# A cross-attention, state-space and feed-forward kernel: the loads for the first two tiles of the modulation stage leave a wait for TensorE's count of turned tiles

## What is computed

```
xt = ln(x)
scores = (xt Wq)(ctx Wk)^T / sqrt(32)        # 4 heads, top 32 of 3202 kept, softmax over these
c_t    = (mean over heads of attn) (ctx Wv)  # context of each token
h = ln(xt) * (1 + gate * scale_in(c_t)) + gate * shift_in(c_t)    # modulation in
y = s4d(h)                                   # a convolution along the 4096 tokens
y = y * (1 + gate * scale_out(c_t)) + gate * shift_out(c_t)
xt = xt + y;  xt = ln(xt + gelu(ln(xt) W1 + b1) W2 + b2)
x  = x + xt;  out = x + bit_ffn(ln(x))       # quantised layers with a convolution of width 3
```

## Time and profile before

| | us |
|---|---|
| median of 3 runs | 3889.6 (3888.87 to 3891.64) |
| the profiled execution | 3883.47, its span 3881.7 |
| busy in the span: PE, DVE, ACT, POOL | 3191.9, 2952.2, 2275.6, 1625.6 |
| attention ends, modulation's first transpose on TensorE starts | 1809.45 |
| modulation ends, s4d's first VectorE instruction starts | 1979.01 |

### The profile page before, as it was taken

One profiled execution on the slowest core, in us unless ns is written; L12 is line 12 of the kernel. 1 busy time (PEld: TensorE's weight loads), 2 busy tenths in 40 slices (PEclk: granted clock), 3 DMA queues, 4 the chain that ended last, 5 costly groups with the idle time before them and its releaser, 6 DMA issues. The chain is left out here.

```text
span 3881.7 us, 54514 instructions
## 1 busy us (share of the span) xinstructions
PE 3191.9 (82%) x17202; PEld 2127.3 (55%) x17202; DVE 2952.2 (76%) x7412; ACT 2275.6 (59%) x2934; POOL 1625.6 (42%) x1324
## 2 busy tenths in 40 slices
PE   7648758887878578887998777689999999978998
PEld 3224334444444244445865555467777777766776
DVE  7799999999999999996668998434444434468898
ACT  4578778898888698883133333133333223357876
POOL 0025546565555365665810000013332333317775
PEclk9758878788888787888999998899999999989999
DMA  9710000000000000002224333633444333430212
GB/s 321 259 47 11 10 8 10 10 10 10 12 10 10 5 13 10 10 5 83 94 58 98 82 92 82 195 121 126 133 133 133 128 103 117 143 97 15 67 50 70
DMA packets 262025, 290.53 MB, mean 75 GB/s; under 512 B 53264, under 2 KB 175782, under 8 KB 260588
## 3 DMA queue, kind: packets, MB, share of 16 engines
q1 hardware_dynamic: 245320, 262.39, 22.1%
q0 software_dynamic: 3040, 14.94, 1.0%
q10 hardware_dynamic: 13380, 10.00, 0.8%
HBM read 218.82 MB, written 68.45 MB: 74 GB/s over the span
## 5 line engine op out<-in xcount | busy, mean ns | idle before, releaser
L1116 PE MATMUL up<-ctx,attnT 128*128 128x384 f32 (+1 forms) x1664 | 718.8, 588 | 44.0 <-ACT attnT L988 43.9
L1086 PE MATMUL score<-KT,q 64*128 64x512 f32 (+1 forms) x1792 | 386.9, 527 | 330.1 <-ACT S L948 240.1
L849 DVE MAX8 both_wide<-S 128x8 f32<-128x146 f32 (+1 forms) x2816 | 601.2, 295 | 43.8 <-ACT S L948 25.0
L808 POOL TENSOR_TENSOR S<-S 128x512 f32<-128x512 f32 (+1 forms) x224 | 424.5, 1927 | 355.0 <-DVE S L854 355.0
L1116 PEld LDWEIGHTS up<-ctx,attnT 128*128 128x128 f32 (+1 forms) x1664 | 367.6, 231 | 319.6 <-issue 158.8
L854 DVE SCALAR_TENSOR_TENSOR S<-S,both_wide 128x3202 f32<-128x3202 f32 x128 | 472.8, 3756 | 14.6 <-ACT both_wide L979 14.6
L1086 PEld LDWEIGHTS score<-KT,q 64*128 64x128 f32 x1792 | 175.7, 239 | 531.9 <-ACT S L948 396.0
L948 ACT ACTIVATE S<-score 128x1024 f32<-128x1024 f32 (+1 forms) x448 | 403.1, 931 | 91.6 <-PE score L1086 91.1
L2301 DVE TENSOR_TENSOR ff_gelu<-ff_whole,ff_gelu 128x512 fp32r<-128x512 f32 x128 | 100.6, 786 | 417.3 <-ACT ff_gelu L2538 417.3
L957 ACT ACTIVATE both_wide<-S,below 128x3202 bf16<-128x3202 f32 x128 | 379.6, 2966 | 41.3 <-DVE below L889 20.4
L979 ACT ACTIVATE both_wide<-S,ebias 128x3202 f32<-128x3202 f32 x128 | 376.2, 2963 | 23.9 <-DVE S L854 13.5
(11 more groups left out here) (500 smaller groups left out, 6462.3 us busy)
## 6 DMA issues: line engine op xcount, KB each, us to landing
s_hankel<-scratch_K SPq DMA_DIRECT2D x128, 256.0 KB, 4.2
ff_w_low<-scratch_w1l SPq DMA_DIRECT2D x112, 256.0 KB, 2.7
ff_w_low<-scratch_w2l SPq DMA_DIRECT2D x112, 256.0 KB, 2.8
xt_prep<-in_x SPq DMA_DIRECT2D x8, 1024.0 KB
scratch_xt<-xt_prep SPq DMA_DIRECT2D x8, 1024.0 KB, 7.4
both_wide<-in_ffn_w_t POOLq DMA_DIRECT2D x8, 1024.0 KB, 11.2
q<-scratch_qt SPq DMA_DIRECT2D x128, 64.0 KB
mod_xt<-in_x_turned SPq DMA_DIRECT2D x32, 256.0 KB, 2.6
```

The costliest lines, as they stand in the source:

```text
L808: nc.gpsimd.tensor_tensor(S[:, b, 0, chunk(j)], S[:, b, 0, chunk(j)], S[:, b, 1, chunk(j)], ALU.add).then_inc(s["summed01"], 1)
L849: nc.vector.max(cand[:, h, 8 * k:8 * k + 8], S[:, b, h, k * SEG:min((k + 1) * SEG, G)])
L1086: last = nc.tensor.matmul(score[bank(p, j)][:, e, 0:w], lhsT=q[at, b, part, h // 2, :], rhs=KT[at, h // 2, chunk(j)], start=(part == 0), s ...
L1116: last = nc.tensor.matmul(up[:, 0:DV], lhsT=attnT[0:w, e, c - 4 * g, :], rhs=ctx[0:w, c, :], start=(c == 0), stop=(c == GC - 1))
```

## The change

In `load`, the wait for `u_turned` is made for tiles 2 to 31 only. For tiles 0 and 1 it asked for counts 1 and 2, which TensorE's line 1374 alone supplies. No instruction with a duration is added, removed or moved on any engine; one line more stands in the file, so that lines after 1222 have a number higher by one in the changed kernel.

```
         def _(sp):
             def load(m, b):
                 n = 2 * m + b
-                sp.wait_ge(s["u_turned"], n + 1)
+                if n >= 2:
+                    sp.wait_ge(s["u_turned"], n + 1)
                 if n >= TILES - 4:
                     sp.wait_ge(attended["u_stored"], 16 * (n + 2))
                 sp.dma_start(u[:, b], dram["u"][n * P:(n + 1) * P, :]).then_inc(s[f"uin{b}"], 16)
```

## The result

| | before | changed |
|---|---|---|
| median of 15 runs, us | 3889.14 (3885.53 to 3896.27) | 3882.02 (3878.34 to 3887.76) |
| ratio, 95% interval | 1 | 0.9983 (0.9977 to 0.9990) |
| span of the profiled execution, us | 3881.7 | 3879.7 |

What follows compares the result with a forecast made beforehand. The prediction took the bias chain (SyncE's wait, bias transfer, GpSimd, VectorE) to hold TensorE, the bound from there; 5.6 us for the first product plus 0.7 for the clock, 6.3 us, gave 3889.6 - 6.3 = 3883.3 us, range 3879.5 to 3888.2.

Steps and rivals of the forecast that it cites:

- The bound: In front of modulation, SyncE's wait, bias transfer, GpSimd and VectorE hold TensorE's first product; from there TensorE bounds, 4.92 us a tile.
- The first term, 5.6 us: At the start of modulation, TensorE's first product comes at 1811.9 instead of 1817.47, 5.6 us earlier.
- bound of four times for GpSimd: GpSimd's three bias operations beside VectorE's weight operations: even four times slower, they cost at most 3.9 us of slack.
- The slack: VectorE before tile 0's low part: free from 1806.2, it waits for ScalarE's high part until 1811.3, 5.1 us.
- The clock, +0.7 us: TensorE's clock at the first modulation products: the change gains between -0.6 and +2.0 us, taken as +0.7.
- middle case: TensorE's clock at the seam falls and returns after 3.4 us of work at half speed: 1.7 lost, +0.3 us.
- high case: TensorE's clock never falls at the seam, so nothing is lost: +2.0 us.
- The loads in the loop: SyncE's loads from tile 2 on: u of tile 2 arrives in time behind the tables, whose earlier start is worth nothing.
- That the clock stays high: Rival: TensorE's clock stays high at the seam and later stages help, 8 to 9 us gained, 3881 us; chance 0.19.
- That the gain is lost behind the barrier: Rival: another wait takes the place or the barrier swallows the gain, 3888 to 3889.6 us; chance 0.10.
- the slower rival: Rival: table writes slow attention's last 28 products on TensorE; at a factor of 2.5, 14 us more, 3897 us; chance 0.03.
- The signs of being wrong: At the seam: line 1308 starting after 1812, GpSimd's bias past 1809, `up` ending after 1809.5, or no gain at the span's end.

Runs made afterwards that it cites:

- bias-alone kernel: Kernel before, with only the bias transfer issued ahead of the loads of tiles 0 and 1, which keep their wait: ratio 0.9993 to before, seam 166.03 us.
- bias-held kernel: Changed kernel, but SyncE waits for TensorE's first count just ahead of the bias transfer: ratio 0.9990 to the kernel before, seam 166.26 us.
- kernel turned early: Changed kernel, tiles 0 and 1 transposes ahead of attention's last products, ScalarE's tile 0 high part ahead of attention's last copy: 0.9971 and 0.9975 of before.
- tables-held kernel: Changed kernel, but SyncE waits for TensorE's first count ahead of the two table transfers: ratio 0.9979 to the kernel before, seam 162.08 us.
- bias in the middle: Changed kernel, with the bias transfer moved behind the wait for attention's last turned tile: ratio 0.9983 to the kernel before, seam 163.61 us.
- kept-warm: Changed kernel with 12 more transposes of tile 1 between those of tiles 0 and 1: ratio 0.9984 to the kernel before, seam 162.08 us.
- the one with the tables behind tile 2: Kernel before, with the bias ahead of the loads of tiles 0 and 1, and tile 2's load ahead of the tables: ratio 1.0000, seam 169.70 us.

## Why the prediction was right

**The bound.** That the bias chain, and nothing else behind SyncE's wait, held the first product is shown by the bias-alone kernel (2.42 us) from one side and the bias-held kernel (4.92 us) from the other.

**The first term, 5.6 us.** It was worked out as 1817.47 - 1811.9; counted from the end of `up` it is 7.95 - 2.42 = 5.53 us. ScalarE's high part, named as the next late one, is what VectorE waits for. The kernel turned early removes that order, and TensorE's wait goes with it.

**The contention.** The bound of four times for GpSimd was not reached: 2.78 and 2.60 us against 1.25, 2.2 and 2.1 times. But the prediction let VectorE "still stop at 1804.20", and that was wrong: its two-input operation beside them took 2.67 us instead of 1.76, in the kernel before:

```profile
1798.81 1.76 DVE L1330 TENSOR_TENSOR mod_wf_parts<-third_table,mod_wf_parts 128x1536 fp32r<-128x1536 f32 x1
```

From the end of the last sums to the end of the weights VectorE needed 1808.05 - 1794.27 = 13.78 us, against 1804.20 - 1791.53 = 12.67, 1.1 us more. The slack was given as 5.1 us and measured as 5.63, and that this is so close is luck: the 1.1 us came off it, and the low clock at 1792.44, which the prediction did not have, put 1.6 us on. With less of that low clock the tables-held kernel has 5.11 us. The bias in the middle shows both slownesses to come from the overlap: without it 1.25 to 1.27 us, and no change on the path.

**The clock, +0.7 us.** Seam 5.91 less first product 5.53 leaves +0.4, close to the middle case (+0.3), and the tables-held and kept-warm kernels show the high case: 169.49 - 162.08 - 5.53 = +1.9, given as +2.0. The two profiles of the changed kernel give +0.4 both times, and none of that kernel shows the high level kept, so the +0.7 is 0.3 us too much by what was seen. The interval of the ratio is too wide to tell the two apart.

**The loads in the loop.** "Covered" was right for the changed kernel, and not for every order of the queue. I had priced the tables at nothing because GpSimd has 39.5 us to spare (45.0 in the changed kernel). Their other side, 2 MB in the queue in front of TensorE's next `u`, was seen and not priced: the bias-alone kernel pays 2.1 us for it, the one with the tables behind tile 2 pays 3.0 us and the clock on top. The removed wait is worth its full 5.9 us because it frees both. Two times in the working were off without harm. The three transfers ahead of the bias went with `x_read`, 3.7 us before it (1790.63 against 1794.29), and not together with it. And the tables reached GpSimd 1812.96 - 1804.62 = 8.34 us after their issue, not 11.6: counted from the end of `up` GpSimd started on them 11.3 us earlier than before, where the prediction has 7.7 (its own issue times differ by 8).

**The rivals.** That the clock stays high was seen in two kernels that are near the changed one, in none of its own profiles. That the gain is lost behind the barrier is spoken against by the ratio over 15 executions, 6.6 us with 5.9 at the seam. The pair of profiles (1902.31 against 1902.69 us behind the seam) agrees by luck: the changed kernel's second profile had 1907.87 us there. Attention's last 28 products took 9.39 us with the 2 MB beside them, as before: the slower rival had no effect at all.

**The signs of being wrong.** Read as they stand, two of them came up: line 1309 (1308 before) started at 1815.62, after 1812, and `up` ended at 1813.81, later than 1809.5. Both stem from the 4.29 us by which this execution is late at that place. Counted from the end of `up`, the low part started 1.81 us behind it, where the prediction has 1811.3 - 1809.52 = 1.8. A sign given as a time of the whole profile can't be told from such a shift; one given as a distance from a common instruction can.

What stays open: why attention and the stages behind the seam differ by several us between executions of one kernel (1901 to 1909 us from s4d's start on), and what decides whether the clock falls over 1.61 us of idle. Neither was studied.

## What to carry to other kernels

A wait in a queue is worth what the most urgent transfer behind it is worth: look past the transfers whose condition it is to those that stand behind it in program order. Here a wait written for the loads of two tiles, which nobody missed, held an 8 KB transfer that the next stage's first product needed. Before moving a large transfer that itself nobody waits for, look which small ones will then stand behind it. And where single executions scatter by more than the change, compare a stretch between two instructions that both kernels have, not the spans.

## What the runs showed of the hardware

GpSimd could use a transfer of 8 KB 1.80 us after its issue with nothing issued in the 19 us before it (bias held), and 3.04 us after with four transfers of 192 to 256 KB issued in the 1.8 us before it (kernel before). Both times count until GpSimd's first operation on it.

Two-input operations on GpSimd and VectorE slowed each other: 1.25 to 2.78 us on the one, 1.76 to 2.67 us on the other. The Trainium skill (GPSIMD Engine Reference, section "Specifications") states contention between GpSimd and VectorE instructions with two SBUF inputs. The trace agrees, and GpSimd's first operation, beside VectorE's one-input cast, kept its 1.29 us. The rows also fit the two engines taking turns by whole operations. GpSimd's second operation began at 1800.02, while line 1329 ran until 1801.67: 1.65 us of it and 1.25 of its own make 2.90, against 2.78. Line 1331 on VectorE began at 1801.74, 1.06 us before that ended: 1.06 + 1.76 = 2.82, against 2.67. GpSimd's third began 1.47 us before the end of line 1331: 1.47 + 1.25 = 2.72, against 2.60. This is read from the rows and was not tested by itself.

The same idle time of 1.61 us on TensorE cost the high clock in both profiles of the changed kernel (in the first, low from 1816.1 to 1819.5), and not in that of the kernel with the tables held.
